# Attention values in two versions per key tile, the rest of the far terms by sums of probabilities, and block transposes on VectorE

## The reference, cut to what matters

```python
pos = jnp.arange(S)
idx = jnp.clip(pos[None, :] - pos[:, None], -MAX_REL, MAX_REL) + MAX_REL
rk2 = rel_k[idx]
rv2 = rel_v[idx]
attn = softmax((einsum('bhqd,bhkd->bhqk', q, k) + einsum('bhqd,qkd->bhqk', q, rk2)) / scale)
w1 = einsum('bhqk,bhkd->bhqd', attn, v)
w2 = einsum('bhqk,qkd->bhqd', attn, rv2)
out = (w1 + w2).transpose(0, 2, 1, 3).reshape(B, S, E) @ Wo.T + bo
```

## Time and profile before

| | us |
|---|---|
| median of 3 runs | 2548.1 (2545.23 to 2548.66) |
| the profiled execution, its time | 2547.91 |
| its span, first to last instruction | 2546.1 |

### The profile page before, as it was taken

How to read it: one execution, slowest core, us unless ns; L and a number is a source line. 1 busy time by engine, 2 the same in 40 slices (tenths; PEclk the granted TensorE clock), 3 DMA queues, 4 the chain that set the end, 5 groups by cost and what they waited for, 6 DMA issues and landing times. The chain is left out here.

```text
span 2546.1 us, 96676 instructions
## 1 busy us (share of the span) xinstructions
PE 2275.5 (89%) x37544; PEld 1602.9 (63%) x37544; DVE 1902.7 (75%) x3734; ACT 1585.2 (62%) x3954; POOL 1037.4 (41%) x1350
## 2 busy tenths in 40 slices
PE   5763499999999999999999999879999996999999
PEld 3442377777777767776777777646656664666665
DVE  5664488888888878887888888647776764787777
ACT  3442377777778878887878778647767762222222
POOL 5665345555554555455545554300000002333332
PEclk8887699999999999999999999979999997999999
DMA  6887245555555554554554544300101001111010
GB/s 193 269 259 224 80 107 118 112 116 115 124 112 116 118 120 111 116 116 113 110 119 114 122 110 100 59 26 26 37 25 37 25 30 63 29 29 33 25 37 17
DMA packets 568111, 242.65 MB, mean 95 GB/s; under 512 B 462278, under 2 KB 531526, under 8 KB 563142
## 3 DMA queue, kind: packets, MB, share of 16 engines
q1 hardware_dynamic: 567750, 237.52, 37.3%
HBM read 134.13 MB, written 103.29 MB: 93 GB/s over the span
## 5 line engine op out<-in xcount | busy, mean ns | idle before, releaser
L884 ACT ACTIVATE a_probs<-a_bank_s,a_neg_max 128x512 f32<-128x512 f32 x1024 | 693.7, 683 | 182.0 <-DVE a_neg_max L819 179.9
L819 DVE TENSOR_REDUCE a_neg_max<-a_bank_s 128x2 f32<-128x1024 f32 x512 | 627.0, 1225 | 55.5 <-DVE a_bank_s L798 3.2
L671 PE MATMUL a_bank_pt<-a_ident,a_probs 128*128 128x128 f32 x4096 | 568.4, 281 | 6.2 <-issue 4.3
L671 PEld LDWEIGHTS a_bank_pt<-a_ident,a_probs 128*128 128x128 f32 x4096 | 442.6, 142 | 110.6 <-issue 62.3
L864 ACT ACTIVATE a_probs_t<-a_bank_pt 128x512 f32<-128x512 f32 x512 | 305.6, 597 | 168.3 <-PE a_bank_pt L671 158.9
L805 DVE COPY a_probs_t<-a_bank_pt 128x512 f32<-128x512 f32 x512 | 349.9, 683 | 28.9 <-PE a_bank_pt L671 24.1
L660 PE MATMUL a_bank_s<-a_k,a_q 48*32 48x512 bf16 (+15 forms) x4096 | 271.1, 286 | 71.3 <-DMA a_kl<-scr_parts 66.6
L697 PE MATMUL a_bank_o<-a_probs_t,a_v 128*32 128x32 f32 (+2 forms) x15872 | 304.5, 226 | 5.0 <-issue 4.8
L697 PEld LDWEIGHTS a_bank_o<-a_probs_t,a_v 128*32 128x32 f32 x15872 | 243.4, 111 | 61.6 <-ACT a_probs_t L864 40.2
L660 PE MATMUL a_bank_s<-a_kl,a_q 48*32 48x204 bf16 (+14 forms) x3840 | 241.9, 265 | 23.8 <-ACT a_probs L884 18.3
L1543 ACT ACTIVATE e_gate<-e_bank_g 128x512 f32<-128x512 f32 x144 | 86.0, 597 | 275.7 <-PE e_bank_g L1482 275.7
(11 more groups left out here) (161 smaller groups left out, 3594.0 us busy)
## 6 DMA issues: line engine op xcount, KB each, us to landing
scr_probs<-a_probs SPq DMA_DIRECT2D x256, 144.0 KB, 5.6
a_raw<-scr_qr SPq DMA_DIRECT2D x256, 96.0 KB
scr_qr<-p_qr SPq DMA_DIRECT2D x64, 320.0 KB, 2.5
a_feat<-scr_probs SPq DMA_DIRECT2D x256, 78.0 KB
scr_parts<-p_sp SPq DMA_DIRECT2D x144, 128.0 KB, 2.8
a_left<-scr_probs SPq DMA_DIRECT2D x256, 64.0 KB, 2.5
a_q<-scr_parts SPq DMA_DIRECT2D x32, 192.0 KB
a_k<-scr_parts SPq DMA_DIRECT2D x32, 192.0 KB
```

The lines of the kernel that those rows point to most:

```text
L671: ins = nc.tensor.transpose(b_pt[bank_of(job)][:, 0, t * P:(t + 1) * P], probs[(u - 1) % 4][:, j, MAX_REL + t * P:MAX_REL + (t + 1) * P], ...
L819: nc.vector.tensor_reduce(neg_max[:, 2 * pair:2 * pair + 2], b_s[:, 2 * pair:2 * pair + 2, :], AX.X, ALU.max, negate=True).then_inc(max_ok, 1)
L884: nc.scalar.activation(probs[u % 4][:, j, MAX_REL:MAX_REL + S], b_s[:, j, :], ACT.Exp, bias=neg_max[:, j:j + 1], accum_out=sums[:, t, j, u ...
```

## The change

EDGES has two entries instead of six. A key tile now has one version of V for queries to its right (all its keys are taken as far left) and one for queries at or to the left of it (all taken as far right); the matmuls are no longer cut. What this gets wrong is the far-left keys in the query's own tile and, for the first query block, at the end of the tile before. It is made good by `moved`: for each query the sum of its probabilities over those keys, times the difference of the two far terms. A reduce on DVE makes these sums, twice per tile (at the end of units with u % 4 == 3 and u % 4 == 1). POOL widens them (moved_wide) as it does the inverse. The 16 small matmuls that spread inv_wide go; inv_wide and moved_wide are instead transposed in blocks of 32x32 by DVE at the end of the units with u % 4 == 0. `scale` adds moved_t before it multiplies.

```diff
-EDGES = (P,) + tuple(n * QBLK - MAX_REL for n in range(1, NQB + 1)) + (0,)
+EDGES = (P, 0)
...
-        probs = [sb(f"probs{s}", [P, NQB, S + 2 * MAX_REL]) for s in range(4)]
+        all_probs = sb("probs", [P, NJ, NQB, S + 2 * MAX_REL])
+        probs = [all_probs[:, k] for k in range(NJ)]
...
 def attended(b, u, s):
                 for kt in range(NT):
-                    if kt == t:
-                        parts = [(n * QBLK, (n + 1) * QBLK, EDGES.index(max(n * QBLK - MAX_REL, 0)))
-                                 for n in range(NQB)]
-                    elif kt == t - 1:
-                        parts = [(0, QBLK, EDGES.index(P - MAX_REL)), (QBLK, P, EDGES.index(P))]
-                    else:
-                        parts = [(0, P, EDGES.index(P if kt < t else 0))]
-                    for lo, hi, edge in parts:
-                        for j in range(NJ):
...
+                    edge = EDGES.index(P if kt < t else 0)
+                    for j in range(NJ):
+                        out = b_o[32 * j:32 * j + 32, 0, t * P:(t + 1) * P].rearrange("p (i q) -> p i q", q=QBLK)
+                        ins = nc.tensor.matmul(out, V[s][:, V_SLOTS.index((edge, kt)), j, hh * 24:hh * 24 + 32],
+                                               probs_t[u % 2][:, :, kt * P + j * QBLK:kt * P + (j + 1) * QBLK],
+                                               start=first, stop=False, skip_group_check=True)
...
 def features(b, u):
-                pe.wait_ge(wide_ok, b * NT + u // 4 - 1)
                 bank_free(pe, b, nxt)
-                nc.tensor.transpose(b_pt[bank_of(nxt)][:, 0, 0:P], flat[:, (FC - 1) * P:], ident[:])
-                for i in range(NQB):
-                    for g in range(NJ):
-                        ins = nc.tensor.matmul(b_pt[bank_of(nxt)][g * QBLK:(g + 1) * QBLK, 0, P + i * QBLK:P + (i + 1) * QBLK],
...
+                ins = nc.tensor.transpose(b_pt[bank_of(nxt)][:, 0, 0:P], flat[:, (FC - 1) * P:], ident[:])
...
+            def sum_moved(b, t, units):
+                v.sem_inc(sum_ok, 1)
+                for i in range(NQB):
+                    a, z = (t * P - MAX_REL, t * P) if i == 0 else (t * P, t * P + i * QBLK - MAX_REL)
+                    if a >= 0:
+                        nc.vector.tensor_reduce(moved[:, t, i, units], all_probs[:, units, i, MAX_REL + a:MAX_REL + z],
+                                                AX.X, ALU.add)
...
                     if u % 4 == 1 and not (first if u == 1 else tail):
+                        sum_moved(b, t, slice(2, 4))
...
+                    if u % 4 == 3 and not tail:
+                        need(v, exp_ok, b, 4 * UNITS, 4 * (u - 1))
+                        need(v, wide_ok, b, 2 * NT, 2 * (u // 4 + 1 - NT))
+                        sum_moved(b, u // 4, slice(0, 2))
                     if u % 4 == 0 and not (first if u < 8 else tail):
...
-                        nc.vector.tensor_copy(last_t[:, t].rearrange("p a q -> p (a q)"),
-                                              b_pt[bank_of(job)][:, 0, 0:2 * P]).then_inc(pt_ev[bank_of(job)], 1)
+                        nc.vector.tensor_copy(last_t[:, t], b_pt[bank_of(job)][:, 0, 0:P]).then_inc(pt_ev[bank_of(job)], 1)
+                        v.wait_ge(wide_ok, b * 2 * NT + 2 * (u // 4 - 1))
+                        nc.vector.transpose(inv_t[:, t], inv_wide[:].rearrange("p h d -> p (h d)"))
+                        nc.vector.transpose(moved_t[:, t], moved_wide[:].rearrange("p h d -> p (h d)")).then_inc(spread_ok, 1)
...
 POOL, make_feature:
+                need(g, spread_ok, b, NT, t)
+                nc.gpsimd.tensor_tensor(moved_wide[:], moved[:, t].rearrange("p i (h o) -> p (i h) o", o=1)
+                                        .to_broadcast([P, H, HD]), left_less_right[:], ALU.mult).then_inc(wide_ok, 1)
...
 POOL, scale:
-                job_read(g, b, (4, "features", 1))
-                nc.gpsimd.tensor_tensor(o_sb[:], o_sb[:], last_t[:, :, 1, :], ALU.mult).then_inc(att_ok, 1)
+                g.wait_ge(spread_ok, b * NT)
+                nc.gpsimd.tensor_tensor(o_sb[:], o_sb[:], moved_t[:], ALU.add).then_inc(both_ok, 1)
+                g.wait_ge(both_ok, b)
+                nc.gpsimd.tensor_tensor(o_sb[:], o_sb[:], inv_t[:], ALU.mult).then_inc(att_ok, 1)
```

More of the change, by code:

```diff
@@ L387 @@
 FC = H * NF // P
-V_SLOTS = [(e, kt) for kt in range(NT) for e in range(NE) if not (kt == NT - 1 and EDGES[e] >= P - MAX_REL)]
+V_SLOTS = [(e, kt) for kt in range(NT) for e in range(NE) if not (kt == NT - 1 and EDGES[e])]
 JOBS = [(u, "probs", j) for u in range(UNITS) for j in range(NJ)]
@@ L462, in attend @@
         inv_wide, ones = sb("inv_wide", [P, H, HD]), sb("ones", [P, H, HD])
+        moved = sb("moved", [P, NT, NQB, NJ])
+        moved_wide, left_less_right = sb("moved_wide", [P, H, HD]), sb("left_less_right", [P, H, HD])
         band = sb("band", [P, WIN])
@@ L468, in attend @@
         feat_t = sb("feat_t", [P, FC - 1, P])
-        last_t = sb("last_t", [P, NT, 2, P])
+        last_t = sb("last_t", [P, NT, P])
+        inv_t, moved_t = sb("inv_t", [P, NT, P]), sb("moved_t", [P, NT, P])
         y_in = sb("y_in", [P, NT, E])
@@ L491, in attend @@
         f_in, l_in, feat_ok = sem("f_in"), sem("l_in"), sem("feat_ok")
-        inv_ok, wide_ok, att_ok = sem("inv_ok"), sem("wide_ok"), sem("att_ok")
+        inv_ok, wide_ok, spread_ok, sum_ok, att_ok = (sem(n) for n in ("inv_ok", "wide_ok", "spread_ok", "sum_ok", "att_ok"))
+        far_ok, both_ok = sem("far_ok"), sem("both_ok")
         y_ld, y_ok, y_st = sem("y_ld"), sem("y_ok"), sem("y_st")
@@ L686, in attended @@
                 for kt in range(NT):
-                    if kt == t:
-                        parts = [(n * QBLK, (n + 1) * QBLK, EDGES.index(max(n * QBLK - MAX_REL, 0)))
-                                 for n in range(NQB)]
-                    elif kt == t - 1:
-                        parts = [(0, QBLK, EDGES.index(P - MAX_REL)), (QBLK, P, EDGES.index(P))]
-                    else:
-                        parts = [(0, P, EDGES.index(P if kt < t else 0))]
-                    for lo, hi, edge in parts:
-                        for j in range(NJ):
[L696 to L701, removed]
+                    edge = EDGES.index(P if kt < t else 0)
[4 more added lines that the diff above has]
+                                               start=first, stop=False, skip_group_check=True)
+                    first = False
                 ins.then_inc(av_ps, 1)
@@ L733, in weigh @@
                     ins = nc.tensor.matmul(b_w[:, 0, t * P:(t + 1) * P], feat_w[:, c, :],
-                                           feat_t[:, c, :] if c < FC - 1 else last_t[:, t, 0, :],
+                                           feat_t[:, c, :] if c < FC - 1 else last_t[:, t, :],
                                            start=c == 0, stop=c == FC - 1)
@@ L783, in _ @@
             v.wait_ge(const_in, N_CONST_IN)
+            for lo, hi, own, other in ((0, E // NQB, 1, 0), (E // NQB, E, 0, 1)):
+                nc.vector.tensor_tensor(left_less_right[:].rearrange("p h d -> p (h d)")[:, lo:hi], v_bias[:, own, lo:hi],
+                                        v_bias[:, other, lo:hi], ALU.subtract).then_inc(far_ok, 1)
+            nc.vector.memset(moved[:], 0.0)
+            v.wait_ge(far_ok, 2)
             nc.vector.tensor_tensor(v_bias[:], v_bias[:], v_in[:, 0:1, :].to_broadcast([P, NE, E]),
@@ L826, in row @@
                         need(v, exp_ok, b, 4 * UNITS, 4 * (u - 1))
-                        need(v, wide_ok, b, NT, u // 4 - 1)
+                        sum_moved(b, t, slice(2, 4))
+                        need(v, wide_ok, b, 2 * NT, 2 * (u // 4 - 1))
                         nc.vector.reciprocal(inv[:], sums[:, t].rearrange("p i h -> p (i h)")).then_inc(inv_ok, 1)
+                    if u % 4 == 3 and not tail:
+                        need(v, exp_ok, b, 4 * UNITS, 4 * (u - 1))
+                        need(v, wide_ok, b, 2 * NT, 2 * (u // 4 + 1 - NT))
+                        sum_moved(b, u // 4, slice(0, 2))
                     if u % 4 == 0 and not (first if u < 8 else tail):
@@ L833, in row @@
                         if t == 0:
+                            need(v, w_ps, b, NT, 0)
                             need(v, att_ok, b, 1, 0)
-                        nc.vector.tensor_copy(last_t[:, t].rearrange("p a q -> p (a q)"),
-                                              b_pt[bank_of(job)][:, 0, 0:2 * P]).then_inc(pt_ev[bank_of(job)], 1)
+                        nc.vector.tensor_copy(last_t[:, t], b_pt[bank_of(job)][:, 0, 0:P]).then_inc(pt_ev[bank_of(job)], 1)
+                        v.wait_ge(wide_ok, b * 2 * NT + 2 * (u // 4 - 1))
+                        nc.vector.transpose(inv_t[:, t], inv_wide[:].rearrange("p h d -> p (h d)"))
+                        nc.vector.transpose(moved_t[:, t], moved_wide[:].rearrange("p h d -> p (h d)")).then_inc(spread_ok, 1)
                     if u == 6 and not first:
```

3 lines of the change are left out of this document (removed).

## The result

The changed kernel takes 2554.9 us (median of 13 runs, 2546.2 to 2561.4) against 2547.0 for the one before (13 runs, 2542.5 to 2561.5): ratio 1.0028, 95% interval 1.0015 to 1.0041. It is slower by 0.3%, not by the forecast 0.7%. Its profiled run fell low in that spread: 2548.5 us, span 2546.7, against 2547.9 and 2546.1. In each later experiment the kernel before was timed again beside the changed one (medians 2551.8, 2548.6 and 2544.7 us), so kernels of different experiments are compared by their ratios to it and not by their times.

What follows compares the result with a forecast made beforehand. DVE was taken as the bound through most of a tile, with ACT and PE finishing its path. 2547.9 + 20.8 (path) + 0.7 (stage end) - 4 (instructions) gave 2565 us, 0.7% slower; range 2546 to 2591.

Steps and rivals of the forecast that it cites:

- What bounds the kernel, and the path of a tile: Attention stage: DVE through units 2, 3 and 0, ACT through feat_t, PE through unit 1; plain units 4.30 us.
- PE as the pace setter: Rival: PE bounds the stage, a tile saves 0.59 us, 2506 us, weak form 2527; together chance 0.12.
- Values on PE, 0.05 us: Values block with 16 wide matmuls per unit: 0.05 us shorter, counting only in units 3 and 1.
- inv_wide, last_t and the transposes at nothing: Unit 0: removed PE matmuls, narrower last_t copy and two DVE transposes (0.42 us) leave the path unchanged, transposes hidden.
- sum_moved: DVE reduces, 0.60 us a call: hidden at unit 1's end, paid at unit 3's, net +0.30 to +0.40 for tiles 0-2.
- My 0.10 of hole: DVE's idle 0.10 us before the add at the end of a tile's fourth unit, subtracted from the reduces' price.
- Tile 3's 0.20: Reduces at a row's last tile, where the next row's start may idle DVE: counted as half, +0.20 us.
- 20.8: Path growth over 16 rows at 1.30 us a row, us added to the stage.
- Instructions, -4: PE's shorter stream removes waits for instructions from the second row on: 4 us off, bounds 0 and twice that.
- slower: Sign of the whole change: slower by more than 0.2%, chance 0.73; within 0.14, faster 0.13.
- The rival without handover: Each short DVE reduce costs its whole duration, 0.93 us a call instead of 0.60: 2586 us, chance 0.10.
- Whole matmuls with the full 0.21: Rival: PE's values block shortens by 0.21 us, a tile grows only 0.10: 2546 us, no change, chance 0.15.

Runs made afterwards that it cites:

- the filled: Changed kernel with 2 spare PE matmuls ahead of features and 1 behind the next scores, per tile: 2541.8 us, ratio 0.9971.
- call in unit 1 only: Changed kernel without the sums' reduces at the end of unit 3, those at the end of unit 1 kept: 2524.5 us, ratio 0.9909.
- halved: Changed kernel with each whole values matmul cut into two of 64 columns, 32 matmuls in a unit: 2562.1 us, ratio 1.0040.
- whole values only: Kernel before with 16 whole values matmuls in every unit and no sums, some far terms left wrong: 2519.5 us, ratio 0.9869.
- no sums: Changed kernel without the eight short reduces per tile, moved staying zero: 2519.6 us, ratio 0.9878.
- half cut: Changed kernel with heads 0 and 1 of each group in cut matmuls, heads 2 and 3 whole, reduces only in unit 1: 2524.9 us, ratio 0.9903.
- half cut, filled: The half cut kernel with 2 and 1 spare PE matmuls per tile around features: 2526.2 us, ratio 0.9922.

## Why the prediction was wrong in size, and right in sign by luck

- *What bounds the kernel, and the path of a tile*: right. Plain units stay at 4.30 to 4.34, and the filled and the unfilled kernel have the same regular row. PE as the pace setter would have brought 0.39 us a tile for the inv_wide matmuls; the kernel with them on PE has the same regular row.
- *Values on PE, 0.05 us*: mis-sized. 0.09 to 0.10 from the block's start to the next instruction, twice a tile on the path: 0.61 us a row, where the sum held about 0.3.
- *inv_wide, last_t and the transposes at nothing*: right for the path (0.01 us a row). Their side effect, a bare wait of 0.49 us on PE and the clock, was not in the sum.
- *sum_moved*: a call of 0.55 instead of 0.60; the call in unit 1 hidden, as forecast; the call in unit 3 paid. By tile its price is 0.35, 0.56 and 0.45 (unit 3, 7 and 11 after against the kernel with the call in unit 1 only). My 0.10 of hole exists in tiles 0 and 2 and not in tile 1. Tile 3's 0.20 didn't come: unit 15 has 5.02 after and 5.09 without the call. The path grew by 12.5 us instead of 20.8; of the 8.3, some 5 are the values block and the rest this.
- *Instructions, -4*: this is the step that failed. I took one group of "<- issue" waits and bounded the whole by twice that. All groups together were 13.9 us, beyond that bound of 8, all went, and the uneven excess fell by 16.2. Had I summed them over all lines, the view of the earlier trace rows would have given 14. Its other lines are:

```profile
PE a_bank_pt L671 <- issue: 4.3, 9, 1.4
PE a_bank_s L660 <- issue: 3.1, 4, 1.1
PE a_bank_pt L711 <- issue: 1.0, 2, 0.6
PE a_bank_w L733 <- issue: 0.7, 1, 0.7
```

- *The clock*: not in the sum at all. 3 us in the profiled pair; 13 to 14.5 us by the ratios of the changed kernel and those with the wait filled. It is also what makes the kernel slower: with the waits filled the same change is 0.3% faster than the kernel before (0.9971). That "slower" came true is therefore luck, since the path's +12.5 and the -16.2 alone would not have given it.
- *The rival without handover* is out: four reduces that last 0.30, 0.24, 0.17 and 0.18 us one by one, 0.89 together, stand in 0.55. The section of the Trainium skill that the prediction cites (VectorE: DVE Perf Modes, "The DRAIN you can't avoid") goes on to say that a next op that is not held starts earlier; the prediction left that out, and the trace agrees with it, as the earlier trace rows did. For the block transposes the same page of the Trainium skill ("The three transpose paths") has 311 ns for bf16; here f32 took 301 and 270.
- *Whole matmuls with the full 0.21*: no, 0.09. To the next instruction a block takes 1.01 us whole, 1.03 halved and 1.10 with the slices of 32 queries, with the same columns each time: nearly all of its length goes with the columns, and most of the 0.09 with the narrow slices, not with the count of records.

With 14 for the instructions and the values at 0.09 the sum would have been some 2550. The misses partly cancel: the path was taken 8 us too high, the instructions' gain 12 too low, and the clock's 13, an estimate from ratios, were missing.

**What went ahead of the falls, and what stays open.** PE's waits in the 5 us ahead of a fall, first the one at 758.0 in the changed kernel, then those at 1194.0 and 368.0 in the kernel before:

```profile
PE a_bank_pt L708 <- ACT a_probs_t L876: 0.5, 1, 0.5
PE a_bank_pt L676 <- ACT a_feat_t L908: 0.5, 1, 0.5
```

```profile
PE a_bank_s L660 <- issue: 1.1, 1, 1.1
```

```profile
PE a_bank_s L660 <- DMA a_kl<-scr_parts: 2.5, 1, 2.5
```

Five of the six falls in the changed kernel and four of the six in the halved one come right behind the pair of waits for probs_t and feat_t. The other three there, and all nine in the kernels before (3), whole values only (2), no sums (2), half cut (1) and half cut, filled (1), come at a longer wait, of 1.1 to 4.4 us, for K, for instructions or for probs. With the call in unit 3 the pair is some 0.55 and 0.49 us; without it (no sums, call in unit 1 only, half cut) 0.35 and 0.49, and no fall follows it. The four variants with the wait for feat_t filled have none either. So the falls that the change added come with that pair, in which the missing matmuls and the longer wait beside the call in unit 3 meet. How many fewer there are without the call is not settled: the median clock of no sums (5 runs) and of the call in unit 1 only (6 runs) is 0.956, between 0.953 and the 0.958 of the filled kernels, and that of half cut (6 runs) 0.96. What stays open too is why 5 of 59 such pairs were followed by a fall and the others not, and equally why not every long wait is; each count is from one profile.

## What to carry to other kernels

Add up the waits for instructions over all lines before pricing a change that shortens an engine's stream: they can outweigh the path. Work that is added to the bounding engine is free only where that engine idles in that unit; look for such a hole (here unit 1) and leave undone what falls outside it. Removing hidden work from PE was not neutral here, where it left a bare wait: compare the granted clock over all runs, look at what PE waited for ahead of each fall, and size what fills the wait by its records.

## What the runs showed of the hardware

- A block transpose of 128x128 f32 on DVE lasts 0.27 to 0.30 us, and the next instruction starts 0.19 to 0.22 after it.
- Four reduces of 24 to 152 elements take 0.55 us from the first start to the add behind them.
- A values block of 32 records of 128 columns takes 1.08 us, one of 64 records of 64 columns 1.10, one of 64 records with slices of 32, 96 and 128 columns 1.17.
- In the twelve kernels PE has no wait for instructions up to 22012 matmul records in 1260 us, 3.9 us at 23678 and 13.9 us at 28996.
- A fall of the granted clock to 1.2 GHz lasts 3.4 or 6.8 us here; a values block then takes 1.66 to 1.93 us. One came behind two waits of PE of 0.5 us each.
